# Fusing the row maximum into ScalarE, turning 15 key tiles on VectorE and doubling q on GpSimd in an attention and mixture-of-experts kernel

## What is computed

```
Q, K, V  = xn @ W_Q + b_Q, xn @ W_K + b_K, xn @ W_V + b_V      # 16 heads of 64
scores   = Q @ K.T / sqrt(64)                                   # 2048 x 2048 a head and batch
attn     = softmax(scores)                                      # exp(s - max) / sum
out      = sum over heads of (attn @ V) @ W_O + b_O
routed   = top 8 of 32 experts a token, weighted (sigmoid router)
shared   = silu(xn @ G) * (xn @ U) @ D
```

## Time and profile before

| | |
|---|---|
| median of 3 runs | 3157.94 us (3156.8 to 3158.17) |
| span of the profiled execution | 3342.4 us |
| PE busy | 3124.5 us (93%) |
| DVE busy | 2625.2 us (79%) |
| POOL busy | 2101.7 us (63%) |
| ACT busy | 1965.3 us (59%) |
| projections, routing, v | from 0 to about 750 us |
| experts | from about 750 to 960 us |
| attention | from 964.87 us (first score matmul) to the end |

### The profile page before, as it was taken

One profiled execution on the slowest core, in us unless ns is written; L12 is line 12 of the kernel. 1 busy time (PEld: TensorE's weight loads), 2 busy tenths in 40 slices (PEclk: granted clock), 3 DMA queues, 4 the chain that ended last, 5 costly groups with the idle time before them and its releaser, 6 DMA issues.

```text
span 3342.4 us, 53910 instructions
## 1 busy us (share of the span) xinstructions
PE 3124.5 (93%) x13443; PEld 1609.9 (48%) x13444; DVE 2625.2 (79%) x2773; ACT 1965.3 (59%) x3797; POOL 2101.7 (63%) x2148
## 2 busy tenths in 40 slices
PE   7965659999979999999999999999999999999998
PEld 3433323445544555555555555455555555555554
DVE  8600013433359999999999999999999999999995
ACT  4500003203447777777777777677777777777775
POOL 4877771001126777777777777667777777777776
PEclk9987769999989999999999999999999999999999
DMA  8810017776658988879899888898888889888987
GB/s 315 326 66 23 17 42 283 252 178 209 229 155 227 227 226 215 220 202 222 225 223 225 215 217 204 210 253 221 225 220 217 214 209 221 225 223 218 219 204 182
DMA packets 318996, 685.52 MB, mean 205 GB/s; under 512 B 120749, under 2 KB 170680, under 8 KB 318544
## 3 DMA queue, kind: packets, MB, share of 16 engines
q1 hardware_dynamic: 289744, 626.48, 71.1%
q0 software_dynamic: 29184, 58.22, 5.4%
HBM read 198.37 MB, written 159.51 MB: 107 GB/s over the span
## 4 chain that ended last, share of the span: by engine, by line
PE 64%; DMA 2%; SPq 1%; DVE 1%; issue 1%; POOL 1%; ACT 0%; POOLq 0%; ACTq 0%
PE at_ps L1110 26%; PE at_ps L1142 25%; PE at_ps L1157 8%; PE at_ps L1123 5%; DMA at_moved<-at_blocks 1%; SPq L934 1%; DVE at_half_max L1239 1%; DVE at_blocks L1256 1%; DMA out<-ahead_acc 0%; POOL at_moved L1052 0%; POOL ahead_acc L1067 0%; ACT at_prob L1193 0%; DMA ahead_acc<-base 0%; SPq L783 0%; POOL ahead_acc L1044 0%
## 5 line engine op out<-in xcount | busy, mean ns | idle before, releaser
L1193 ACT ACTIVATE at_prob<-at_ps,at_neg_max 128x1024 f32<-128x1024 f32 x1024 | 1150.4, 1123 | 323.7 <-DVE at_neg_max L1244 284.5
L1239 DVE TENSOR_REDUCE at_half_max<-at_ps 128x1 f32<-128x1024 f32 x1024 | 1202.2, 1215 | 26.6 <-PE at_ps L1110 25.2
L1256 DVE STREAM_TRANSPOSE at_blocks<-at_prob 128x1792 f32<-128x1792 f32 x512 | 1043.1, 2037 | 5.9 <-DMA at_moved<-at_blocks 3.2
L1052 POOL COPY at_moved<-at_blocks 32x1792 f32<-32x1792 f32 x512 | 858.2, 1676 | 159.2 <-DVE at_blocks L1256 61.0
L1110 PE MATMUL at_ps<-ahead_k_hl,ahead_q_hh 128*128 128x512 f32 x2048 | 854.1, 417 | 22.9 <-ACT at_prob L1193 16.2
L1142 PE MATMUL at_ps<-at_moved,at_v 128*64 128x512 f32 x3584 | 863.2, 595 | 6.9 <-DMA at_moved<-at_blocks 6.9
L1110 PE MATMUL at_ps<-ahead_k_hl,ahead_q_ll 128*128 128x512 f32 x2048 | 809.4, 395 | 0.0
L1067 POOL TENSOR_TENSOR ahead_acc<-ahead_acc,at_scaled 128x256 f32<-128x256 f32 x512 | 376.5, 735 | 228.0 <-ACT at_scaled L1205 105.6
L1110 PEld LDWEIGHTS at_ps<-ahead_k_hl,ahead_q_hh 128*128 128x128 f32 x2048 | 388.6, 190 | 96.9 <-ACT at_prob L1193 24.2
L1142 PEld LDWEIGHTS at_ps<-at_moved,at_v 128*64 128x64 f32 x3584 | 262.5, 138 | 354.5 <-issue 299.6
L1205 ACT ACTIVATE at_scaled<-at_ps,at_inv 128x256 f32<-128x256 f32 x512 | 242.9, 474 | 316.2 <-PE at_ps L1157 263.0
(11 more groups left out here) (112 smaller groups left out, 2783.7 us busy)
## 6 DMA issues: line engine op xcount, KB each, us to landing
at_moved<-at_blocks SPq DMA_DIRECT2D x1536, 224.0 KB
ahead_k_hl<-k_parts SPq DMA_DIRECT2D x64, 512.0 KB, 8.2
ahead_q_hh<-q_parts SPq DMA_DIRECT2D x128, 256.0 KB, 4.3
ahead_q_ll<-q_parts SPq DMA_DIRECT2D x128, 256.0 KB, 6.1
xbuf<-pr_zeros SPq DMA_DIRECT2D x32, 512.0 KB, 3.9
q_parts<-pr_part_hi SPq DMA_DIRECT2D x64, 256.0 KB
q_parts<-pr_part_lo SPq DMA_DIRECT2D x64, 256.0 KB
k_parts<-pr_part_hi SPq DMA_DIRECT2D x64, 256.0 KB
```

Source lines behind the costliest of these rows:

```text
L1052: nc.gpsimd.tensor_copy(moved[r * 32:(r + 1) * 32, parity, r, :, :, :], blocks[r * 32:(r + 1) * 32, parity, r, :, :, :]).then_inc(diag_don ...
L1193: nc.scalar.activation(prob[:, i % 2, half * 1024:(half + 1) * 1024], ps[:, banks[0]:banks[1], :].rearrange("p b c -> p (b c)"), ACT.Exp, ...
L1239: nc.vector.tensor_reduce(half_max[:, i % 2, half:half + 1], ps[:, banks[0]:banks[1], :], AX.XY, ALU.max).then_inc(max_step, 1)
L1256: nc.vector.transpose(blocks[:, parity, :, j, :, :].rearrange("p c t k -> p t c k"), prob[:, (s["s"] - 1) % 2, 0:MOVED * P].rearrange("p ( ...
```

## The change

Six edits go together.

1. **Maximum.** DVE's reduce of each half writes the negated maximum (`neg_half`), and DVE no longer joins the two. ACT does, ahead of the late exp, with two activations of one element a partition: `rise` = relu(-neg_late + neg_early), then `neg_max` = -rise + neg_early. Each is waited for.
2. **Scale.** The factor 1/8 goes from exp into wq and bq, which DVE multiplies once, early in the program; PE waits for that (`q_scaled`) before its first q or k projection.
3. **Key tiles.** `MOVED = 15`, `TURNED = 1`: DVE turns 15 tiles and PE one. The exchange's DMAs and POOL's block copies carry 15 tiles in place of 14, ACT's `take` copies 128 columns in place of 256.
4. **q.** `load_q` fills only partitions 0 to 63. POOL copies them to partitions 64 to 127, high and low part (`double_q`), and PE waits for `q_doubled` in place of `q_loaded`. POOL does this for the next group at the start of its slots 3, 7, 11 and 15, ahead of that slot's add.
5. **k.** k's rows lie in DRAM as 64 high rows and then 64 low rows a head, so the store of a pair of heads takes 4 DMAs of 64 rows in place of 2 of 128.
6. Semaphore counts follow.

```diff
@@ project_and_route @@
+        STORES = (32, 64)
                     for part, src in ((0, part_hi), (1, part_lo)):
-                        sp.dma_start(dst[part, pair * P:(pair + 1) * P, bass.ds(c * CH, CH)],
-                                     src[:, u % 4, :].bitcast(F32)).then_inc(qk_stored[u % 4], 16)
+                        if is_key:
+                            for h in range(2):
+                                row = (2 * pair + h) * P + part * DH
+                                sp.dma_start(scr["k"][row:row + DH, bass.ds(c * CH, CH)],
+                                             src[h * DH:(h + 1) * DH, u % 4, :].bitcast(F32)
+                                             ).then_inc(qk_stored[u % 4], 16)
...
+            nc.vector.tensor_scalar(wq[:, :, :], wq[:, :, :], DH ** -0.5, None, ALU.mult)
+            nc.vector.tensor_scalar(bq[:, :], bq[:, :], DH ** -0.5, None, ALU.mult).then_inc(q_scaled, 1)
...
+            pe.wait_ge(q_scaled, 1)
@@ attend @@
-MOVED = 14
+MOVED = 15
-FIRST_TILES = (14, 15, 13, 12)
+FIRST_TILES = (15, 14, 13, 12)
...
-        sp.dma_start(dst[:, g % 2, :].bitcast(F32), src.unsqueeze(1).to_broadcast([DH, 2, CH])
-                     ).then_inc(start["q_loaded"][g % 2], 16)
+        sp.dma_start(dst[0:DH, g % 2, :].bitcast(F32), src).then_inc(start["q_loaded"][g % 2], 16)
...
+            def double_q(head, g):
+
+                wait_apart(pool, q_loaded[g % 2], 32 * (head * 2 + g // 2) + 32, pool_waits)
+                for q in (q_hh, q_ll):
+                    nc.gpsimd.tensor_copy(q[DH:P, g % 2, :], q[0:DH, g % 2, :].bitcast(F32)).then_inc(q_doubled, 1)
+                wait_apart(pool, q_doubled, 2 * (head * GROUPS + g) + 2, pool_waits)
...
+                if i == 0 and b == 0 and isinstance(h, int) and h == 0:
+                    double_q(0, 0)
+                if i < TILES and i % GT == GT - 1 and not (b == B - 1 and isinstance(h, int) and h == H - 1 and i == TILES - 1):
+                    last = i // GT == GROUPS - 1
+                    double_q(s["head"] + last, (i // GT + 1) % GROUPS)
...
-                        pe.wait_ge(q_loaded[g % 2], 32 * (head * 2 + g // 2) + 32)
+                        pe.wait_ge(q_doubled, 2 * (head * GROUPS + g) + 2)
...
-                    if place == 0 and n == 2:
+                    if place == 0 and n == TURNED:
...
                 if half == 1:
+                    neg_early, neg_late = neg_half[:, i % 2, 0:1], neg_half[:, i % 2, 1:2]
+                    act.wait_ge(half_done, 2 * tile + 2)
+                    nc.scalar.activation(rise[:, i % 2:i % 2 + 1], neg_late, ACT.Relu, bias=neg_early, scale=-1.0
+                                         ).then_inc(rise_done, 1)
+                    act.wait_ge(rise_done, tile + 1)
+                    nc.scalar.activation(neg_max[:, i % 2:i % 2 + 1], rise[:, i % 2:i % 2 + 1], ACT.Identity,
+                                         bias=neg_early, scale=-1.0).then_inc(max_done, 1)
...
-                nc.vector.tensor_reduce(half_max[:, i % 2, half:half + 1], ps[:, banks[0]:banks[1], :],
-                                        AX.XY, ALU.max).then_inc(max_step, 1)
-                if half == 1:
-                    dve.wait_ge(max_step, 2 * tile + 2)
-                    wait_pos(dve, early_exp, tile - 1)
-                    nc.vector.tensor_scalar(neg_max[:, i % 2:i % 2 + 1], half_max[:, i % 2, 0:1],
-                                            half_max[:, i % 2, 1:2], -(DH ** -0.5), ALU.max, ALU.mult
-                                            ).then_inc(max_done, 1)
+                nc.vector.tensor_reduce(neg_half[:, i % 2, half:half + 1], ps[:, banks[0]:banks[1], :],
+                                        AX.XY, ALU.max, negate=True).then_inc(half_done, 1)
```

More of the change, by code:

```diff
@@ L145, in project_and_route @@
         counts_done = m.sem("counts_done")
+        q_scaled = m.sem("q_scaled")
         counts_read = m.sem("counts_read")
@@ L237, in _ @@
             for n in range(4):
-                sp.wait_ge(qk_stored[n], NC * H // 4 * 32)
+                sp.wait_ge(qk_stored[n], NC * H // 4 * STORES[n % 2])
             for n in range(4):
@@ L810, in attend @@
         acc = start["acc"]
-        half_max = m.sb("half_max", [P, 2, 2])
+        neg_half = m.sb("neg_half", [P, 2, 2])
+        rise = m.sb("rise", [P, 2])
         neg_max = m.sb("neg_max", [P, 2])
@@ L824, in attend @@
         wo_loaded = m.sems("wo_loaded", 2)
+        q_doubled = m.sem("q_doubled")
         early_scored = m.sem("early_scored")
         late_scored = m.sem("late_scored")
-        max_step = m.sem("max_step")
+        half_done = m.sem("half_done")
+        rise_done = m.sem("rise_done")
         max_done = m.sem("max_done")
@@ L1194, in exponent @@
                                      ps[:, banks[0]:banks[1], :].rearrange("p b c -> p (b c)"),
-                                     ACT.Exp, bias=neg_max[:, i % 2:i % 2 + 1], scale=DH ** -0.5,
+                                     ACT.Exp, bias=neg_max[:, i % 2:i % 2 + 1],
                                      accum_out=half_sum[:, i % TILES, half:half + 1]).then_inc(done, 1)
```

8 lines of the change are left out of this document (5 added, 3 removed).

## The result

| | before | after |
|---|---|---|
| median of 4 runs | 3158.06 us (3156.8 to 3158.32) | 4003.82 us (4002.44 to 4005.47) |
| ratio | | 1.2675 [1.2657, 1.2693] |
| profiled execution: its own time | not given | 4002.84 us |
| profiled execution: span | 3342.4 us | 4001.2 us |
| first score matmul of attention | 964.87 us | 826.35 us |

A forecast was written before the change was run, and what follows sets the result against it. PE was taken to bound the kernel, busy without a break in attention. 3158 (median) + 613 (PE-POOL loop) + 240 (clock) + 5 (before attention) - 184 (profile correction) = 3832 us; range 3560 to 4140 us.

The forecast's parts named there:

- The loop: In attention PE and POOL wait on each other through q's copies once a group: 91.9 us a head against 72.7.
- The clock: In attention PE runs at 1.2 GHz for a while after each pause: 7.5 us a head, 240 us.
- SP has room beside PE's matmuls: Before attention, 128 more k-store DMAs of half the size on SP cost 3 us, ends 0 and 42.
- From the profile to the time: Profiled span exceeds the median by 184 us, put into 256 indirect DMAs; attention's 256 gathers save another 184 us unprofiled.
- the smaller correction: Alternative saving on attention's gathers outside the profiler, from 620 ns against 976 ns a DMA: 91 us, forecast 93 higher.
- 0.4 us would just fit: ACT's two one-element activations in attention: 0.4 us fits if PE never stops; 0.94 overruns by 0.3 to 0.4 a slot.
- the rival where q's copies come in time: In attention PE never waits for POOL and DVE's 4.39 us bounds the slot: 79 us less, 3084 us; chance 4%.
- 613: Attention's added time from PE and POOL waiting on each other: 19.15 us more a head, over 32 heads, in us.
- 5 was 39 too low: The term before attention, DVE's scaling of wq and the extra k-store DMAs: 5 us together.
- The two rivals on the clock: After attention's pauses the clock stays up (3592 us, chance 10%) or stays down (5300 us, chance 2%).
- Only POOL's added work shows: In attention POOL catches up between groups; PE waits 1.83 us a group, 234 us: 3397 us, chance 7%.

The follow-up runs named there:

- x4: The kernel after, with 18 useless matmuls on PE ahead of its wait for q's copies in slots 4, 8 and 12: 3827.86 us.
- x5: The kernel before, with only k's stores split into 4 DMAs of 64 rows a pair of heads, DRAM rows unchanged: 3199.05 us.
- x12: The kernel before, with only ACT's copy of the finished weighted values moved ahead of the early half's exp: 3148.57 us.
- x7: The kernel before with ACT joining the maxima, the scale in wq and 15 tiles on DVE; q and k loaded and stored as before: 3212.13 us.
- x1: The kernel after, but q is loaded by DMA into both partition halves and POOL copies none of it: 3267.07 us.

## Why the prediction was right, and where it was not

**The loop (edit 4), right.** It was predicted that PE may not begin slots 4, 8, 12 and 0 without POOL, that POOL's chain hangs on PE's slot 5, and that it runs from that slot's add over the block copies and gathers. The trace has PE waiting 574.2 us for POOL's q copies, 123 times. Term by term: the add of slot 5 comes 3.39 us into the slot (3.38 predicted); from there to the end of the q copies are 16.26 us (14.70 + 0.43 + 1.4 = 16.53). A q copy takes 0.60 us, and the second starts 0.56 behind the first: 1.16 for both and no wait between them, which is the 0.24 us too much. In x4, with the clock taken out, a head has 92.48 us; 91.9 were predicted. The four groups agree one by one: 24.4 and 24.3 us on average for the starts behind slots 7 and 11 (24.3 predicted), 23.8 behind slot 3 (23.5) and 19.9 behind slot 15 (19.9). The pauses are 5 to 6 us and not 6 to 7, since the slots ahead of them were longer than 4.36 us each.

**The clock, mechanism right, size too large.** Predicted were 7.5 us a head, 240 us. x4 gives 98.0 - 92.5 = 5.5 us a head, 176 us. On average the kernel after is longer than x4 by 2.0, 1.7 and 2.3 us in slots 4, 8 and 12, near the 2.0 each. In slot 0 it is 0.6 us, where 1.5 were put: the 1.5 are there, but in 13 of 32 heads only. The pause ahead of it is 1.8 us, not the 2.4 expected, and why the clock falls behind one such pause and not behind the next stays open. These four make 6.6 us, and 5.5 of them reach the head, since some of the other slots are shorter than in x4. The Trainium skill (TensorE: Matmul & The Clock Gate, section on the HAM clock gate) calls the ramp under 1% of a span for modelling. That does not hold for this kernel, which pauses once a group: it is 176 of 4004 us, 4.4%. The Trainium skill's section on oscillation, of the same page, describes a kernel that pays for the ramp anew at every wait. Behind the three long pauses the trace agrees, with windows at 0.50 and 0.56.

**Edit 5, wrong by a factor of fifteen.** "SP has room beside PE's matmuls, so I take 3 us", with 0 and 42 us as ends. x5 shows 44 us, just outside. The row gave the 0.33 us of the DMA instruction alone, not the time that SP needs from one issue to the next, and I never set SP's period for a pair of units against PE's. From the trace of before alone it would have come out close, and no more: 0.51 us from store to store (the next one behind that of the earlier trace rows begins at 601.64), six stores for a q and a k unit, 3.06 us against 3.42. What makes SP the bound is that a split store takes 0.67 us: 3.94 are measured.

**From the profile to the time, wrong.** "So I put the 184 us into the 256 indirect DMAs", and another 184 us for the gathers: none of it holds. The indirect DMAs take 975 ns in the kernel after, as in the earlier trace rows, and its span (4001.2 us) is its own time (4002.84 us). The Trainium skill's figure of some 620 ns for a DMA issued by GpSimd alone (SBUF — State Buffer, on its two separate sides) was the base of the smaller correction, 91 us. No run here shows that figure. The smaller correction falls with the larger one. The profiled execution of the kernel before was long in another place. Windows over the shared expert's matmuls, before and, second, of x12, and between them ACT's largest wait in the former:

```profile
141.00:481.00 340.00, 205.65 (x513) 109.77 (x511) 30.39 (x46) 31.91 (x44) 246.37 (x296) 0.78 0.13 43
```

```profile
ACT pr_score L337 <- remote: 239.4, 19, 42.7
```

```profile
142.00:314.00 172.00, 167.86 (x514) 97.92 (x512) 30.88 (x47) 32.37 (x45) 124.49 (x149) 0.99 0.23 82
```

The same 513 or so matmuls take 340 us in the one and 172 in the other, since ACT's activations of silu stood for 239 us behind something that the profile only calls remote. None of the twelve experiments has this in its trace, x12 starts attention at 784.32 us, and the timed runs have no room for it. What held ACT in that one execution stays open. So the part ahead of attention is 42 us longer after than in x12, the k stores again, and not 139 us shorter as the two profiles side by side would have it.

**Edits 1 and 3, right for the forecast, too kind for the rival.** They were costed at nothing inside the loop, where x4's head shows no more than 0.6 us for whatever was left out. "0.4 us would just fit", while 0.94 would overrun by 0.3 to 0.4 a slot: the activations take 0.58 us, in between, and with them the late exp starts 0.3 to 0.4 us later. Without the loop that costs 57 us (x7), against the gain of 79 us in the rival where q's copies come in time. DVE's 4.39 us a slot were a little low as well: in x7 it is busy for 1881 us over 424 slots, 4.44 us each. That rival, 3084 us, would have been wrong even with POOL in time: x1 says 3267.

**The sum.** With the measured sizes it is 3158 + 613 + 176 + 44 = 3991 us, 13 below what was measured. Mine was 3832, since -184 was wrong by the whole, 5 was 39 too low, and 240 was 64 too high. Without the correction it would have been 4016 us, 12 above what was measured, and part of that nearness is luck: the term of the clock and that of the k stores are wrong in opposite directions. That 4004 lies in the range owes something to its width, 580 us. The two rivals on the clock are out: it neither stays up nor stays down. "Only POOL's added work shows" (3397) is out as well: it has PE wait for 234 us, and the waits are 574 us.

## What to carry to other kernels

When a step moves onto an engine with an in-order queue, find its place there in the trace and follow what stands ahead of it back to its start: if that is the waiting engine's own work, the two form a loop, and the price is the loop's length and the clock behind each pause, not the step's 1.2 us. Set the time that each queue and engine needs per unit of work, gaps included, beside that of the engine that bounds the stage, and ask at which point of the unit a moved step is due, since a mean share (ACT's 55%) doesn't tell. Take a profiled span that is far from the timed runs apart by stage before you make a correction out of it. And look at all lengths of a slot, not only at their median, when a cost may come in every second head.
